# Expert stages of an eight-stage network: every token through all eight experts, or tokens sorted into tiles of 256 and sent only to their two

## Chip, cores and metric

One Trainium2 chip, one of its cores. The metric is the device time of one launch, in microseconds (us); the execution whose profile is shown lasted 3942.5 us from its first to its last instruction. A core has TensorE (PE, matrix products; PEld is its weight load), VectorE (DVE), ScalarE (ACT), GpSimd (POOL) and SyncE (SP, which here only issues transfers).

## What is computed

The input is 4 batches of 1024 tokens of 128 values. The reference is a chain of eight stages, each added to the running residual after a layer norm:

```python
x = x + attn_a(layernorm(x))         # stage 0, attention with relative positions
x = x + experts(layernorm(x))        # stage 1
x = x + mamba(layernorm(x))          # stage 2
x = x + experts(layernorm(x))        # stage 3, the same weights
x = x + sparse_attention(layernorm(x))
x = x + ffn(layernorm(x))
x = x + delta_rule(layernorm(x))
x = x + ffn(layernorm(x))

def experts(x):                       # E = 8 experts, 128 -> 2*256 -> 128, K = 2
    probs = softmax(einsum('bsh,eh->bse', x, router_w))
    weights, indices = top_k(probs, 2)
    weights = weights / (weights.sum(-1) + 1e-06)
    gate, up = split(einsum('bsh,ehi->bsei', x, w13))
    y = einsum('bsei,eih->bseh', silu(gate) * up, w2)
    return sum over the two chosen experts of weights * y
```

## The kernel before

The kernel runs the stages one after the other, each as a block of five instruction streams (one for each engine) that meet in semaphores; at the end of a block all engines meet. The residual stays in SBUF for the whole kernel, as 32 tiles of 128 tokens. Only stages 1 and 3 (`moe_stage`, called twice) and the very first loads are touched by the change.

All products of the expert stages are made of 16-bit halves: a 32-bit value is split into a high and a low f16 part, and `product_of_halves` (its matmuls are on L246) adds three matmuls: high by high, high by low, low by high.

`moe_stage` before: the tokens are taken in 8 chunks of 512, and each chunk goes through all 8 experts: 64 units. One unit is

- on PE, `up(j, 0)` and `up(j, 1)`: 12 matmuls of 512 columns (gate and value, two blocks of 128 hidden channels, three products each), then `down(j)`: 24 matmuls of 128 columns;
- on ACT, twice: the Silu of the gate (L1226) and the high half of the hidden values (`keep`, L1234);
- on DVE, twice: the product of gate and value (L1313, "exact"), and four times the weighted addition into the residual (L1324); the weight of an expert that a token didn't choose is zero;
- on POOL, twice: the low half of the hidden values (L1250).

`schedule()` is one list of pieces that every engine walks in the same order, each taking its own. `ahead(j)` slips the preparation of later batches (norm, transposes `turn`, router products `logits`, `choose`) and the splitting of the expert weights (`split`) between the units, so that the first unit starts soon after the stage does. `next_moments` takes the norm's moments for the next stage near the end. The block ends when the last addition is made.

`Net.load_rest` issues the loads that nothing at the kernel's very start needs, on SP's queue, ahead of the transfers of stage 0 (`load_psi` L654, `store_phi` L661, `store` L676, `load_phi` L669, `assemble` L691, in this order).

Of the kernel before, what the change touches and what calls it, by code (L numbers as in the profile page):

```python
# [10 lines left out]
F32 = mybir.dt.float32  # L11
BF16 = mybir.dt.bfloat16
F16 = mybir.dt.float16
U32 = mybir.dt.uint32
ALU = mybir.AluOpType
# [3 lines left out]
P = 128  # L19
# [32 lines left out]
class Net:  # L52
# [978 lines left out]
EB = HIDDEN_E // P  # L1031


def moe_stage(nc, net, name):

    with ExitStack() as stack:
        def sbuf(what, shape, dtype=F32):
            return stack.enter_context(nc.sbuf_tensor(f"{name}_{what}", shape, dtype))  # L1040

        xn = sbuf("xn", [P, TILES, P])
        xT = sbuf("xT", [P, B * T])
        probs = sbuf("probs", [P, TILES, EXPERTS])
# [3 lines left out]
        weights = sbuf("weights", [P, TILES, EXPERTS])  # L1048
# [4 lines left out]
        gate_sb = sbuf("gate", [P, 3, BANK])  # L1053
        exact_sb = sbuf("exact", [P, 3, BANK])
        hidden = sbuf("hidden", [P, 3, EB, 2, BANK], F16)
        xT_halves = sbuf("xT_halves", [P, 2, B * T], F16)
        w13_halves = sbuf("w13_halves", [P, 2, EXPERTS, 2 * HIDDEN_E], F16)
        w2_halves = sbuf("w2_halves", [P, 2, EXPERTS, EB, P], F16)
        w13 = sbuf("w13", [P, EXPERTS, 2 * HIDDEN_E])
        w2 = sbuf("w2", [P, EXPERTS, EB, P])  # L1060
        ps = stack.enter_context(nc.psum_tensor(f"{name}_ps", [P, 8, BANK], F32))
        norm = Norm(net, sbuf, (), xn, xT)
        (tokens_high, tokens_low, weights_high, weights_low, routed, shifted, raised, gate_full, value_full,
         gated, exact_made, hidden_high, hidden_low, out_full, added, step) = net.signals(
            "tokens_high tokens_low weights_high weights_low routed shifted raised gate_full value_full "
            "gated exact_made hidden_high hidden_low out_full added step")
        turned = net.signals("turned_even turned_odd")
        featured = net.signals("featured_even featured_odd")
        chunk = lambda c: slice(c * BANK, (c + 1) * BANK)
        outs = [ps[:, 6, :], ps[:, 7, :]]  # L1070
        units = CHUNKS * EXPERTS


        loads = ((0, 1), (1, 2), (2, 4), (4, EXPERTS))
        weights_in = net.signals("w_first_in w_second_in w_third_in w_rest_in")
        load_of = lambda e_: next(n for n, (_, end) in enumerate(loads) if e_ < end)

        def ahead(j):

            if j < 2:  # L1080
                yield from ([("logits", 0), ("raise", 0)], [("choose", 0, 1)])[j]
            if j + 2 < EXPERTS:
                yield "split", j + 2
            b = j // (2 * EXPERTS) + 1
            at = j % (2 * EXPERTS) - (6 if b == 1 else 2)
            if b < B:
                yield from {0: [("moments", b, 0)], 1: [("moments", b, 1)], 2: [("root", b)], 3: [("apply", b, 0)],
                            4: [("apply", b, 1)], 5: [("turn", b, 0)], 6: [("turn", b, 1)],
                            7: [("logits", b), ("raise", b)], 8: [("choose", b, 0)],
                            9: [("choose", b, 1), ("choose", b, 2)]}.get(at, ())  # L1090

        def schedule():
# [3 lines left out]
            for half in range(HALVES):  # L1096
                yield "apply", 0, half
            yield "split", 0
            yield ("ready",)
            for half in range(HALVES):  # L1100
                yield "turn", 0, half
            yield "split", 1
            for j in range(units + 2):
                if j < units:
                    yield "up", j, 0
                if j in (1, 2):
                    yield "choose", 0, 2 * j - 2
                if 1 <= j <= units:
                    yield "keep", j - 1, 1
                if j == units + 1:  # L1110
                    yield ("next_root",)
                    yield ("next_inverse",)
                if j >= 2:
                    yield "down", j - 2
                if j < units:
                    yield "up", j, 1
                    yield "keep", j, 0
                    if j >= units - 14 and j % 2 == 0 and j < units - 14 + 4 * TAKEN:
                        yield "next_moments", (j - units + 14) // 2
                    yield from ahead(j)  # L1120

        gate_ring, value_ring = Ring([ps[:, i, :] for i in (0, 2, 4)]), Ring([ps[:, i, :] for i in (1, 3, 5)])
        gate_empty = {"gate": gated, "turn": featured[0], "route": shifted}
        value_empty = {"value": exact_made, "turn": featured[1]}
        uses = {}
# [3396 lines left out]
```

## Time and profile before

| | |
|---|---|
| time, 3 runs | 3946.96 us median (3943.35 to 3953.65) |
| the profiled execution's span | 3942.5 us |
| stage 1 | 765.6 to 1054.3 us of the span |
| stage 3 | 1675.6 to 1964.9 us |
| busy over the whole span | PE 82%, DVE 72%, ACT 59%, POOL 31% |

A row of the grouped view gives the line of the kernel, the engine, what is written and read, the shape, the count, the busy time in all and the mean of one in nanoseconds, and then the engine's idle time before these instructions with what ended it. A row of the timeline gives start and length in us; one with a count merges instructions that follow each other, and its length is that of the whole run of them.

### The profile page before, as it was taken

How to read it: one execution, taken by the hardware profiler on the slowest of the kernel's cores; microseconds unless marked ns; L12 is line 12 of the kernel's file. 1: busy time of each engine (PE TensorE's matmuls, PEld its weight loads, DVE VectorE, ACT ScalarE, POOL GpSimd, SP SyncE). 2: the span in 40 equal slices, each digit the busy share in tenths (PEclk: the TensorE clock that was granted, in tenths of full speed). 3: DMA queues.
4: the chain of work that ended last, by engine and by line, in shares of the span. 5: the costliest groups of instructions: out<-in, count | busy, mean ns of one | idle time of the engine just before them, and what ended most of it. 6: DMA issues, size and time to landing. Idle time of an engine off the chain costs nothing. (4 is left out here: it accounts for less than half of the span.)

```text
span 3942.5 us, 87849 instructions
## 1 busy us (share of the span) xinstructions
PE 3249.7 (82%) x36196; PEld 1488.6 (38%) x36256; DVE 2818.9 (72%) x4293; ACT 2313.5 (59%) x3870; POOL 1237.5 (31%) x1018
## 2 busy tenths in 40 slices
PE   6999999899867677689988888887995676776799
PEld 1222222266411122156533333333453555554445
DVE  8898899587679998887746767655445667656643
ACT  3888888766444555266542566665655564543565
POOL 1100100055436776645533000001004565452100
PEclk7999999999967778799999999998997676656799
DMA  4101010100010010010036011101000000000000
GB/s 102 28 9 28 19 21 5 37 1 2 11 32 16 17 32 16 17 33 1 8 69 82 10 36 33 27 23 53 1 8 4 4 4 4 3 4 3 31 6 17
DMA packets 136019, 84.34 MB, mean 21 GB/s; under 512 B 92386, under 2 KB 107539, under 8 KB 135491
## 3 DMA queue, kind: packets, MB, share of 16 engines
q1 hardware_dynamic: 132870, 74.45, 8.7%
q0 software_dynamic: 2688, 4.20, 0.6%
q8 instruction: 289, 4.73, 0.5%
q14 instruction: 108, 0.88, 0.1%
q10 hardware_dynamic: 64, 0.07, 0.0%
HBM read 46.97 MB, written 18.33 MB: 17 GB/s over the span
## 5 line engine op out<-in xcount | busy, mean ns | idle before, releaser
L989 DVE TENSOR_REDUCE attn_peak_halves<-attn_ps 128x2 f32<-128x1024 f32 x512 | 601.5, 1218 | 58.5 <-PE attn_ps L820 50.7
L942 ACT ACTIVATE attn_weights<-attn_ps 128x512 f32<-128x512 f32 x1024 | 531.0, 601 | 101.4 <-PE attn_ps L848 101.3
L2974 DVE TENSOR_REDUCE sparse_peak<-sparse_ps 128x4 f32<-128x1024 f32 x256 | 309.6, 1223 | 136.3 <-PE sparse_ps L2600 134.5
L1250 POOL TENSOR_TENSOR moe_hidden<-moe_exact,moe_hidden 128x512 f16<-128x512 f32 x256 | 296.7, 1162 | 330.7 <-ACT moe_hidden L1234 322.0
L3672 POOL TENSOR_TENSOR delta_q<-delta_q,delta_weighted 128x512 f32<-128x512 f32 x240 | 324.1, 1377 | 235.4 <-ACT delta_weighted L4066 235.3
L2827 ACT ACTIVATE sparse_weights<-sparse_ps 128x512 f32<-128x512 f32 (+1 forms) x512 | 272.0, 585 | 173.8 <-PE sparse_ps L2667 87.9
L246 PE MATMUL moe_ps<-moe_xT_halves,moe_w_halves 128*128 128x512 f16 x1536 | 363.8, 384 | 9.4 <-DVE moe_w_halves L1267 5.9
L1772 POOL TENSOR_TENSOR mamba_out_c<-mamba_states,mamba_c_rep 128x1024 f32<-128x1024 f32 x128 | 301.4, 2367 | 176.8 <-DVE mamba_states L1839 138.5
L848 PE MATMUL attn_ps<-attn_q_stack,attn_k_stack 50*128 50x512 f16 x1024 | 321.9, 386 | 29.9 <-ACT attn_weights L942 7.1
L246 PE MATMUL ffn_ps<-ffn_layers,ffn_h_halves 128*128 128x512 f16 x1536 | 334.5, 379 | 3.6 <-ACT ffn_gate L3219 3.6
L1558 PE MATMUL mamba_ps<-mamba_stack,mamba_spread 96*128 96x512 bf16 x512 | 196.2, 493 | 157.3 <-ACT mamba_decays L1726 85.7
L1839 DVE TENSOR_TENSOR_SCAN mamba_states<-mamba_decays,mamba_ps 128x1024 f32<-128x1024 f32 x128 | 292.7, 2287 | 26.3 <-ACT mamba_decays L1726 10.1
L820 PE MATMUL attn_ps<-attn_k_stack,attn_q_stack 48*128 48x512 f16 x1024 | 271.2, 396 | 13.9 <-DVE attn_peak_halves L989 12.6
L3291 DVE TENSOR_TENSOR ffn_layers<-ffn_exact,ffn_layers 128x512 f16<-128x512 f32 x192 | 132.5, 692 | 204.8 <-ACT ffn_layers L3208 204.3
L860 PE MATMUL attn_ps<-attn_weights,attn_values 128*9 128x512 f32 x2048 | 270.3, 600 | 0.0
L1726 ACT ACTIVATE mamba_decays<-mamba_ps,mamba_rates 128x1024 f32<-128x1024 f32 x128 | 141.9, 1113 | 179.4 <-PE mamba_ps L1558 177.4
L1226 ACT ACTIVATE moe_gate<-moe_ps 128x512 f32<-128x512 f32 x256 | 152.0, 594 | 138.4 <-PE moe_ps L246 134.4
L1313 DVE SCALAR_TENSOR_TENSOR moe_exact<-moe_ps,moe_gate 128x512 f32<-128x512 f32 x256 | 174.5, 684 | 78.4 <-ACT moe_gate L1226 72.4
L848 PEld LDWEIGHTS attn_ps<-attn_q_stack,attn_k_stack 50*128 50x128 f16 x1024 | 80.6, 94 | 375.1 <-ACT attn_weights L942 284.4
L246 PEld LDWEIGHTS ffn_ps<-ffn_layers,ffn_h_halves 128*128 128x128 f16 x1536 | 149.9, 98 | 184.4 <-issue 4.5
L246 PE MATMUL moe_ps<-moe_w_halves,moe_hidden 128*128 128x128 f16 x3072 | 193.7, 220 | 18.2 <-POOL moe_hidden L1250 13.6
L246 PEld LDWEIGHTS moe_ps<-moe_xT_halves,moe_w_halves 128*128 128x128 f16 x1536 | 145.0, 99 | 164.5 <-DVE moe_w_halves L1267 8.0
(451 smaller groups left out, 6293.4 us busy)
## 6 DMA issues: line engine op xcount, KB each, us to landing
mamba_stack<-mamba_parts SPq DMA_DIRECT2D x96, 128.0 KB, 2.4
sparse_factor<-sp_factor SPq DMA_DIRECT2D x24, 256.0 KB
sp_halves<-sparse_parts SPq DMA_DIRECT2D x8, 512.0 KB, 3.1
ffn_h<-in_h SPq DMA_DIRECT2D x4, 1024.0 KB, 7.9
attn_q_stack<-attn_halves SPq DMA_DIRECT2D x96, 32.0 KB
attn_k_stack<-attn_halves SPq DMA_DIRECT2D x96, 32.0 KB
attn_halves<-attn_hp SPq DMA_DIRECT2D x8, 384.0 KB, 3.1
attn_q_stack<-attn_peak_rows SPq DMA_DIRECT2D x128, 2.0 KB
```

Of the source, the lines that this page charges most:

```text
L246: made = pe.matmul(out, a, b, start=first and i == 0, stop=last and i == 2)
L820: made = pe.matmul(use.slot[:, p, :], q_stack[rows, slot, couple, t * P:(t + 1) * P], k_stack[rows, slot, couple, half_of(keys)], start=Tr ...
L848: pe.matmul(use.slot, k_stack[rows, slot, couple, k * P:(k + 1) * P], q_stack[rows, slot, couple, half_of(half)], start=True, stop=True).t ...
L860: made = pe.matmul(out_acc[32 * h:32 * h + HD + 1, :], values[:, b % 2, k, first + h, :], weights[:, step_no(g, half, k) % 2, h, :], start ...
L942: act.activation(weights[:, at % 2, h, :], use.slot, ACT.Exp).then_inc(*key_act.one())
L989: dve.tensor_reduce(peak_halves[:, turn % PEAKS, keys, at:at + 2], use.slot, AX_X, ALU.max).then_inc(*score_dve.one())
L1250: pool.tensor_tensor(low, exact_sb[:, i % 3, :], hidden[:, i // EB % 3, i % EB, 0, :], ALU.subtract).then_inc(*hidden_low.one())
L1772: pool.tensor_tensor(out_c[:, n % PRODUCTS, :], states[:, n % HELD, :], c_rep[:, b % 2, :], ALU.mult).then_inc(*product_made.one())
L1839: dve.tensor_tensor_scan(states[:, n % HELD, :], decays[:, n % DECAYS, :], mine, 0.0, ALU.mult, ALU.add).then_inc(*scanned.one())
L2827: act.activation(weights[:, at % 2, h, begin:], use.slot[:, begin:], ACT.Exp).then_inc(*key_act.one())
L2974: dve.tensor_reduce(peak[:, at % PEAKS, unit // 2, 4 * r:4 * r + 4], use.slot.rearrange("p h (a k) -> p (h a) k", a=2), AX_X, ALU.max).the ...
L3672: pool.tensor_tensor(so_far, so_far, weighted[:, half, :], ALU.add).then_inc(*long_added.one())
```

## The change

`moe_stage` is rewritten. The tokens are now routed first, in three lots (batch 0; batches 1 and 2; batch 3). For each lot, one matmul against a triangle of ones and further ones against all ones (`rank`) count how many tokens of each expert stand before each token; `place_lot` turns that into a slot number for each of a token's two choices, each expert's list rounded up to tiles of 256 slots, and into a table that names each tile's expert. A lot of n batches has 8n + 7 tiles, whatever the routing, so there are 15 + 23 + 15 = 53 tiles.

POOL writes each tile of 128 tokens (both halves, 512 bytes a token) twice into a sorted list in DRAM with an indirect DMA (`scatter`): 64 a stage. SP loads each tile of the list (128 KB) and stores each tile of results (128 KB). After a lot's results are stored, POOL gathers them with 64 indirect DMAs a stage (`gather`), and DVE adds them into the residual (`combine`).

For one tile, PE transposes the 256 tokens by four products with the identity (`gather_tile`), makes 12 matmuls of 256 columns (`up`) and 12 of 128 (`down`). ACT copies the transposed tokens out of PSUM, makes the Silu, the high half (`high`) and the copy of the result (`keep`). DVE reads the tile's expert from the table into a register (`value_load`), copies that expert's 1536 f16 weights a partition into one of four buffers, and makes the exact product and the low half (`low`), which POOL made before.

`prepare(b)` yields apply and turn of both halves, halve, logits, raise, choose in two parts, at a lot's last batch rank and place, then weigh. In the diff below the first lines stand in `load_rest`, ahead of stage 0's transfers; `copy` and `combine` are DVE's, `scatter` is POOL's.

The core of the diff:

```diff
+        for lot in self.sorted_x:
+            n = lot.shape[0] // SLOTS_E
+            sp.dma_start(lot.rearrange("(n p s) d -> p n (s d)", p=P, s=SB), self.dram["e_zeros"].unsqueeze(1).broadcast_to(
+                [P, n, SB * 2 * P])).then_inc(*self.zeroed.dma())
...
+SLOTS_E = 256
+LOTS = ((0, 1), (1, 3), (3, 4))
+PER_EXPERT = 2 * HIDDEN_E * 2 + EB * P * 2
+lot_tiles = lambda g: (LOTS[g][1] - LOTS[g][0]) * T * 2 // SLOTS_E + EXPERTS - 1
...
         def schedule():
+            yield "moments", 0, 0
+            yield "moments", 0, 1
+            yield "root", 0
+            yield ("prepare_consts",)
+            early = [b for b in range(B) if lot_of(b) < 2]
+            for n, b in enumerate(early):
+                yield from prepare(b)
+                if n == 0:
+                    for other in range(1, B):
+                        yield "moments", other, 0
+                        yield "moments", other, 1
+                        yield "root", other
+                for e_ in range(n * EXPERTS // len(early), (n + 1) * EXPERTS // len(early)):
+                    yield "split", e_
+            late = [piece for b in range(B) if lot_of(b) >= 2 for piece in prepare(b)]
+            yield "gather_tile", 0
+            yield "copy", 0
+            yield "copy", 1
+            total_steps = MOE_TILES + 4
+            for j in range(total_steps):
+                if 1 <= j <= MOE_TILES:
+                    yield "high", j - 1
+                if 3 <= j < MOE_TILES + 3:
+                    yield "keep", j - 3
+                if j + 1 < MOE_TILES:
+                    yield "gather_tile", j + 1
+                if 1 <= j <= MOE_TILES:
+                    yield "low", j - 1
+                if j < MOE_TILES:
+                    yield "up", j
+                if j + 2 < MOE_TILES:
+                    yield "copy", j + 2
+                if 2 <= j < MOE_TILES + 2:
+                    yield "down", j - 2
+                if late and j >= 1:
+                    yield late.pop(0)
+                if j == LOT_STARTS[2] + 2:
+                    for c in range(HALVES * LOTS[0][0], HALVES * LOTS[0][1]):
+                        yield "combine", c
+            for c in range(HALVES * LOTS[0][1], CHUNKS):
+                yield "combine", c
...
+                def copy(j):
...
+                    if j >= HELD_W:
+                        dve.wait_ge(*out_full.at(j - HELD_W + 1))
+                    at = dve.value_load(expert_at[0:1, j:j + 1], min_val=0, max_val=(EXPERTS - 1) * PER_EXPERT)
+                    dve.tensor_copy(held[:, j % HELD_W, :], parts[:, bass.ds(at, PER_EXPERT)]).then_inc(*copied.one())
...
+                def scatter(b):
+                    g = lot_of(b)
+                    pool.wait_ge(*tokens_low.at(b + 1))
+                    pool.wait_ge(*placed.at(g + 1))
+                    for t in range(b * TPB, (b + 1) * TPB):
+                        for k in range(2):
+                            pool.indirect_dma_start(net.sorted_x[g], bass.IndirectOffsetOnAxis(slot_at[:, k, t:t + 1], 0),
+                                                    rows[:, t].rearrange("p h d -> p (h d)"),
+                                                    None).then_inc(*scattered[g].dma())
...
+                def combine(c):
+                    dve.wait_ge(*gathered[c].at(16 * 2 * TPC))
+                    for k in range(2):
+                        for t in range(c * TPC, (c + 1) * TPC):
+                            x = net.residual[:, t, :]
+                            made = dve.scalar_tensor_tensor(x, found[:, t, k, :], share[:, k, t:t + 1], x, ALU.mult, ALU.add)
+                        made.then_inc(*added.one())
+                        dve.wait_ge(*added.now())
```

The lists in DRAM are filled with zeros once, at the kernel's start: three DMAs, 53 tiles of 128 KB, 6.9 MB, in rows of 1 KB.

## Rows read from the trace of the kernel before

**Rows 1.** The page of the profile, its first line.

```profile
span 3942.5 us, 87849 instructions
```

**Rows 2.** Busy time by stretch, the two expert stages; behind the engines PE's granted clock.

```profile
765.60:1054.30 288.70, 269.23 (x2400) 172.28 (x2400) 224.75 (x647) 182.97 (x315) 148.34 (x128) 0.97 0.04 12
1675.60:1964.90 289.30, 269.60 (x2400) 172.85 (x2400) 224.57 (x647) 182.91 (x315) 148.33 (x128) 0.98 0.04 12
```

**Rows 3.** Groups of instructions by line and shape, stage 1.

```profile
L1313 DVE SCALAR_TENSOR_TENSOR moe_exact<-moe_ps,moe_gate 128x512 f32<-128x512 f32 x128 | 87.2, 683 | 38.7 <-ACT moe_gate L1226 35.9 <-PE moe_ps L246 2.0 <-issue 0.2
L1234 ACT ACTIVATE moe_hidden<-moe_exact 128x512 f16<-128x512 f32 x128 | 79.9, 624 | 29.8 <-DVE moe_exact L1313 29.5
L1226 ACT ACTIVATE moe_gate<-moe_ps 128x512 f32<-128x512 f32 x128 | 76.0, 594 | 69.3 <-PE moe_ps L246 67.8 <-DVE moe_exact L1313 1.0
...
L327 DVE TENSOR_SCALAR moe_xn<-residual,w_ln_moments,w_ln_inv 128x128 f32<-128x128 f32 x32 | 14.5, 514 | 0.1
L1226 ACT ACT_TABLE_LOAD x7 | 9.0, 1283 | 0.1
...
L1261 DVE TENSOR_TENSOR moe_xT_halves<-moe_xT,moe_xT_halves 128x512 f16<-128x512 f32 x8 | 5.5, 692 | 3.4 <-ACT moe_xT_halves L1214 3.4
...
L416 ACT COPY moe_xT<-moe_ps 128x512 f32<-128x512 f32 x8 | 4.6, 574 | 0.0
```

**Rows 4.** Timeline of one unit near the end of stage 1.

```profile
1035.08 2.75 PE L246 MATMUL moe_ps<-moe_xT_halves,moe_w_halves 128*128 128x512 f16 x12
...
1035.99 0.60 ACT L1226 ACTIVATE moe_gate<-moe_ps 128x512 f32<-128x512 f32 x1 [1.52 <-PE moe_ps L246]
1036.48 0.62 ACT L1234 ACTIVATE moe_hidden<-moe_exact 128x512 f16<-128x512 f32 x1
1036.68 0.69 DVE L1313 SCALAR_TENSOR_TENSOR moe_exact<-moe_ps,moe_gate 128x512 f32<-128x512 f32 x1 [0.27 <-ACT moe_gate L1226]
...
1039.01 2.75 PE L246 MATMUL moe_ps<-moe_xT_halves,moe_w_halves 128*128 128x512 f16 x12
1039.21 1.12 DVE L1324 SCALAR_TENSOR_TENSOR residual<-moe_ps,moe_weights,residual 128x128 f32<-128x128 f32 x4
```

**Rows 5.** Timeline of stage 1's first 22 us.

```profile
766.61 0.38 DVE L316 BATCH_NORM_AGGREGATE w_ln_moments<-w_ln_stats 128x2 f32<-128x6 f32 x4
...
767.79 0.38 DVE L316 BATCH_NORM_AGGREGATE w_ln_moments<-w_ln_stats 128x2 f32<-128x6 f32 x4
...
768.77 2.14 DVE L327 TENSOR_SCALAR moe_xn<-residual,w_ln_moments,w_ln_inv 128x128 f32<-128x128 f32 x8
...
777.67 1.85 PE L1158 MATMUL moe_ps<-w_router,moe_xT 128*128 128x8 f32 x16
...
786.31 0.22 DVE L1284 TENSOR_REDUCE moe_best<-moe_key 128x8 f32<-128x64 f32 x1
786.56 0.22 DVE L1285 TENSOR_TENSOR moe_chosen<-moe_key,moe_best 128x64 f32<-128x64 f32 x1
```

**Rows 6.** Timeline of POOL in stage 4: the only indirect DMAs of the kernel, two of eight.

```profile
2123.13 1.10 POOL L2424 DMA_INDIRECT sparse_gathered_k<-sp_table_k,sparse_row_at  x1 [15.36 <-DVE sparse_row_at L2966]
2124.54 1.00 POOL L2424 DMA_INDIRECT sparse_gathered_v<-sp_table_v,sparse_row_at  x1 [0.30 <-issue]
```

**Rows 7.** Groups by line and shape on DVE: its widest plain cast between SBUF tensors (stage 0).

```profile
L979 DVE CAST attn_phi_parts<-attn_sums 128x1024 f16<-128x1024 f32 x1 | 0.7, 693 | 0.0
```

**Rows 8.** Timeline of the kernel's start, SP's issues and PE's first scores of stage 0.

```profile
13.41 0.82 SPq L654 DMA_DIRECT2D attn_k_stack<-in_psi  x2
...
38.70 1.04 PE L820 MATMUL attn_ps<-attn_k_stack,attn_q_stack 48*128 48x512 f16 x4
```

**Rows 9.** Busy time by stretch while the residual is loaded; last the GB/s moved.

```profile
8.00:10.00 2.00, 0.00 (x0) 0.00 (x0) 0.75 (x4) 1.26 (x3) 0.00 (x0) 1.00 0.99 391
```

**Rows 10.** Busy time by stretch in stages 4 and 6 (PE's first, its granted clock third from last).

```profile
2220.00:2260.00 40.00, 34.35 (x423) 13.62 (x432) 27.83 (x24) 27.85 (x57) 2.53 (x9) 1.00 0.01 3
3060.00:3100.00 40.00, 24.57 (x1256) 21.26 (x1253) 24.43 (x40) 23.83 (x43) 21.02 (x15) 0.67 0.02 5
```

More of the change, by code:

```diff
@@ new lines, in moe_stage, with prepare @@
+        value_bank = lambda j: ps[:, 3 + j % 2, :]
+        out_bank = ps[:, 5, 0:SB * P]
+        span = lambda g: (LOTS[g][1] - LOTS[g][0]) * TPB
+        member_of = lambda g: member[:, LOTS[g][0] * TPB + g:LOTS[g][1] * TPB + g + 1, :]
+        rank_bank = lambda g: ps[:, 7, 0:(span(g) + 1) * EXPERTS]
+        lot_of_tile = lambda j: next(g for g in range(len(LOTS)) if j < LOT_STARTS[g + 1])
+        def prepare(b):
+            yield "apply", b, 0
+            yield "turn", b, 0
+            yield "apply", b, 1
+            yield "turn", b, 1
+            yield "halve", b
+            yield "logits", b
+            yield "raise", b
+            yield "choose", b, 0
+            yield "choose", b, 1
+            if b + 1 == LOTS[lot_of(b)][1]:
+                yield "rank", lot_of(b)
+                yield "place", lot_of(b)
+            yield "weigh", b
@@ L1111, in schedule @@
+            for c in range(HALVES * LOTS[0][1], CHUNKS):
+                yield "combine", c
+                if c == HALVES * TAKEN - 1:
                     yield ("next_root",)
                     yield ("next_inverse",)
[L1113 to L1120, printed above, removed]
@@ new lines, in gather_tile @@
+                def gather_tile(j):
+                    if j == 0:
+                        pe.wait_ge(*prepared.at(1))
+                    pe.wait_ge(*loaded[j % LOADED].at(16 * (j // LOADED + 1)))
+                    if j:
+                        pe.wait_ge(*taken.at(j))
+                    for half in range(2):
+                        for s in range(SB):
+                            at = half * SLOTS_E + s * P
+                            made = pe.matmul(ps[:, 0, at:at + P], sorted_in[:, j % LOADED, s, half * P:(half + 1) * P],
+                                             ident_half[:], start=True, stop=True)
+                    made.then_inc(*turned_tile.one())
@@ L1239, in _ @@
+                pieces = {"root": lambda b: norm.root(act, b), "prepare_consts": prepare_consts, "split": split, "turn": turn,
+                          "halve": halve, "raise": raise_, "gather_tile": gather_tile, "up": up, "high": high, "keep": keep,
+                          "next_root": lambda: norm.root_next(act)}
                 for piece, *at in schedule():
@@ L1280, in take_best @@
+                    dve.tensor_tensor(batch(left, b), found_, wide(best, b), ALU.subtract).then_inc(*shifted.one())
                 def take_best(b, source, into, top):
@@ L1336, in _ @@
+                          "logits": shift_logits, "choose": choose, "place": place_lot, "weigh": weigh, "copy": copy, "up": up,
+                          "low": low, "combine": combine, "next_inverse": lambda: norm.invert_next(dve)}
                 for piece, *at in schedule():
```

414 lines of the change are left out of this document (248 added, 166 removed).

## The prediction, made before the changed kernel was run

> **What bounds the kernel now.** I read the page first: span 3942.5 us, on one core [rows 1]; the terms below are summed against this span, and the median of the runs shown, 3946.96, is 4.5 above it. Then the busy time by stretch: the two stages that are rewritten take 288.7 and 289.3 us, and PE is busy for 269 of each at a granted clock of 0.97 to 0.98 [rows 2]. Last the timeline of one unit: from one unit's first matmul to the next one's are 3.93 us (1035.08 to 1039.01) with PE never idle [rows 4]. 64 units of 3.93 are 251.5 of the 288.7 us; the rest is the start, and units of the first chunks that wait. So the stages are bound by PE, by its columns: a unit has 12 x 512 + 24 x 128 = 9216, which makes 0.426 ns a column.
>
> **PE's work after.** A tile has 12 x 256 + 12 x 128 + 4 x 128 = 5120 columns, 2.18 us at that rate; 53 tiles are 116 us instead of 251. PE stops being the bound, and the question is what a tile costs elsewhere and how long the new start and end are.
>
> **A tile's period.** The order on ACT is high(j-1), keep(j-3), the copy of the transposed tile j+1, Silu(j). high waits for DVE's exact product, and that for the Silu, so a loop closes over two engines: Silu 0.59, hop 0.09 (1036.59 to 1036.68), exact 0.68, a like hop 0.1, high 0.62, keep, copy 0.57 [rows 3, 4]. keep has 256 columns; I take 0.36 (0.57 less half of what 512 columns cost). That sums to 3.0. But ACT starts its next instruction before the former has ended (1035.99 then 1036.48, 0.49 apart for one of 0.60 [rows 4]); with this for the three that follow without a wait it is 2.7. I take **2.8**. PE (2.18) has slack of 0.6. DVE has exact, the weights' copy and low, a 128x512 subtraction that takes 0.69 [rows 3]. The copy's width isn't in the trace: 1536 elements at the rate of the widest cast (1024 in 0.693 [rows 7]) are 1.04, if a copy among f16 goes no faster, and some 0.55 if twice as fast. That makes 1.9 to 2.4, plus what the register load shows of itself. No row shows one. Its bounds: nothing, since it can run while exact does, and 1.4, the whole pitch of an indirect DMA, the nearest thing in which a sequencer or POOL fetches indices (2123.13 to 2124.54 [rows 6]). I take 0.3 exposed, so DVE stays at or under 2.7 and the loop over ACT sets the period. With both DVE costs at their upper ends DVE needs 2.4 + 1.4 - 0.3 overlap = 3.5, and a tile's period is 3.5.
> The Trainium skill, Runtime: NRT & Kernel Launch, the breakdown of the preamble, gives about 1.3 us for a short series of register loads from HBM; no row here shows one. By it the load would show about 0.6 behind exact, and the sum would stay.
>
> **The start.** Before, the later batches' preparation ran between the units. Now three batches are prepared first, each in a chain that no other work covers. Normalising 2.1, two ACT copies 1.2 with the transposes' latency 0.5, the high half of 1024 columns 1.0 and the low half 1.2 (two of 0.69 in one), router matmuls 1.85 beside them, Exp 0.4, and 17 small DVE operations at a pitch of 0.25 [rows 3, 5]: about 12.3. At a lot's end `rank` and `place` add some 1.5 on PE and 14 operations of 0.2 to 0.3, 5 in all; `weigh` is in the 12.3 or adds 0.8. Moments of batches 1 to 3 are 6 halves of 1.18 [rows 5], 7.1; batch 0's moments and root take 3; the eight experts' splits on DVE (0.69 + 0.42 less overlap) are 8 x 1.03 = 8.2, and 1 is lost on ACT. Sum: 3 + 17.3 + 7.1 + 9.2 + 12.3 + 18.1 = 67, and 3 for the first two copies and the first gate: **70 us** until tile 0's Silu.
>
> **The loop.** 52 periods of 2.8 are **145.6**. The twelve late pieces of batch 3 stand one in a step; a DVE piece costs what it takes above a slack of some 0.7: Exp with two table loads of 1.28 [rows 3] about 2, choose 1.2 and 1.0, place 2.7, halve 0.8, logits 0.9, the others 1.9: **10.5**. The additions of chunks 0 and 1 at step 40 take DVE 2 x 3.5 (eight at 0.28 [rows 4], plus moments 1.2): **6.3** after slack. From the last Silu through exact, high, low, down and keep are **4.2**.
>
> **The end.** The last store is issued and lands in 2.8 (no row shows it; twice an indirect DMA's pitch). Only then can POOL gather lot 2: 16 indirect DMAs at a pitch of 1.35 (1.41 at the pair shown [rows 6], the others are nearer 1.3), 21.6; landing 2; eight additions 2.2: **28.9** with the block's end. Lot 1's 32 gathers (43 us) fit into the 46 between tile 37's store and the last one.
>
> Scatters: lot 0's 16 (21 us) run under the preparation of batch 1 and 2. Lot 1's 32 begin at 63 us and last 43, until 106; tile 15 is wanted at about 70 + 15 x 2.8 + 10 = 122, its load some steps earlier. Hidden, with 8 us to spare; with that cover gone each further us on POOL is one on the stage, and SP, which waits at that load, holds the stores of tiles 9 and later behind it.
>
> A stage: 70 + 145.6 + 10.5 + 6.3 + 4.2 + 28.9 = **265.5**. That saves 23.2 and 23.8.
>
> **The zeros.** 6.9 MB stand on SP's queue between the router's load and `load_psi` (13.41), and behind them wait in order psi, phi, the halves' stores and the stacks, all of stage 0's inputs. The load just before moves 391 GB/s at its best [rows 9]; DRAM to DRAM is not in the trace. 6.9 MB take 18 us at 391 and 35 at half of it; I take 24. PE's first scores run at 38.70 [rows 8], behind transposes for the other batches in PE's order; I estimate that the stacks lie ready up to 6 us before. So stage 0 and all behind it shift by **18** (12 to 35).
>
> **Sum:** 3942.5 - 47.0 + 18 = 3913.5 against its span, 3918 against the median of the runs.
>
> **The rivals.**
> (a) *A tile's period is set by DVE, and the kernel is slower.* DVE goes exact, register load, copy, low in a row. If the load can't run beside exact, or the fetch takes over 1.3, the period passes 3.08, where 52 x 2 x 0.28 eat the whole 29 us. At the upper bound of 3.5: 29 - 73 = 44 slower, 3991. For it: nothing in the trace overlaps a register load with anything; against it: DVE has 0.4 to 0.9 of slack a tile. Chance 0.25.
> (b) *POOL becomes the bound.* While POOL computed, DVE's norm instruction took 0.514 on average against 0.27 alone (2.14 for 8) [rows 3, 5]: the two engines get in each other's way, in the rows at DVE's cost. The copies may do this to POOL's indirect DMAs. If each waits out part of a copy, their pitch goes from 1.35 to 1.9: lot 1's gathers overrun by 15, lot 1's scatters by 9, while the last 16 gathers run beside no copies. 24 a stage, 48 in all: 3966. Chance 0.1.
> The Trainium skill, SBUF — State Buffer, "SBUF: two separate sides", says that a DVE copy in a two-port mode locks GpSimd out of writing the descriptors of its own DMAs. The norm row agrees that the two share something; how it strikes a DMA, no run here shows.
> (c) *PE falls to its lower clock.* A stretch of stage 4 is granted 1.00, one of stage 6, where PE is idle more between its matmuls, 0.67 [rows 10]. The loop leaves PE idle for 0.6 us in every 2.8, where before there was no gap [rows 4], and which of the two it will be like the rows don't say. At the lower level, 1.2 GHz, a tile needs 4.36, so a third of the loop there costs 17 x 1.56 = 27 a stage, 54 in all: 3972. Chance 0.12.
> (d) *No gain and no loss*: the zeros cost 34, the period 2.9: 3942.5 - 36 + 34 = 3940, as runs 3945. Chance 0.13.
> (e) The loop at its lower bound, 2.7 with the zeros at 12: 3913.5 - 10 - 6 = 3897, as runs 3902; this is in the forecast's own spread, 3890 to 3934, chance 0.4.
>
> Within 0.3% (12 us) of the median is what a measurement of this kernel can't tell from no change. The forecast's 0.4 is all faster, and half of (d) and some of (a) to (c) where they strike mildly: faster 0.5, within 0.3% 0.18, slower 0.32. The range runs from 3885 to 4000: above it are (a) with (b) or (c) together, below it a start much shorter than I sum.
>
> **What would show it.** In the trace of the changed kernel: Silu to Silu 2.8 in the middle of the loop, with ACT's high waiting for DVE's exact each time and PE idle 0.5 a tile; stage starts with tile 0's Silu at 70 us; 16 gathers in a row with every other engine idle at the end, 22 us; the first scores of stage 0 at 57 instead of 38.7; granted clock above 0.9 in the loop. Wrong it would be if DVE shows no idle time between exact and low, or an idle of over a us ahead of each copy; if POOL's indirect DMAs are spaced by more than 1.6; or if tile 15 waits for its load.

## The result, and the profile after

The changed kernel took **4106.58 us** (median of 4 runs, 4102.23 to 4108.92) beside 3947.57 for the one before (3943.35 to 3953.65): ratio 1.0403, 95% interval 1.0388 to 1.0418. The forecast was 3918, the range ended at 4000. The profiled execution has a span of 4107.0 us, 164.5 more than [rows 1]. The same kernel then took 3908 to 3910 us in three of four later measurements and 4114 in the fourth; what parts the two outcomes is what the experiments are about. One execution below, of e2 (4050 us, granted clock 0.745 where its neighbours had 0.84), ran in a slower state; it counts in e2's median and not in its ratio.

First the busy time by stretch of the changed kernel, the two expert stages, which answer to [rows 2]; the columns are window, length, PE, PEld, DVE, ACT and POOL busy with instructions, granted clock, DMA share and GB/s.

```profile
785.60:1151.40 365.80, 173.19 (x1615) 139.30 (x1615) 183.26 (x519) 129.81 (x258) 124.89 (x128) 0.69 0.24 71
...
1774.95:2138.70 363.75, 171.26 (x1615) 137.43 (x1615) 182.72 (x516) 129.36 (x258) 124.83 (x128) 0.70 0.24 71
```

The stages are 77.1 and 74.5 us longer than before, where 23 each were to be saved. The first starts 20.0 later (785.6 for 765.6), stage 2 takes 2.3 more, and stages 4 to 7 take 9.3 less (1968.3 for 1977.6), which I can't explain: 20.0 + 77.1 + 2.3 + 74.5 - 9.3 = 164.6. PE's work fell as forecast, from 269 to 173 us; none of the five engines is busy for much more than half of the stage. So the time is idle time. The groups of stage 1, with what ended the idle time ahead of each, answer to [rows 3]:

```profile
L1495 DVE SCALAR_TENSOR_TENSOR moe_exact<-moe_ps,moe_gate 128x512 f32<-128x512 f32 x53 | 36.6, 691 | 92.8 <-ACT moe_gate L1339 50.7 <-issue 32.0 <-PE moe_ps L251 5.1
L1345 ACT CAST moe_hidden<-moe_exact 128x512 f16<-128x512 f32 x53 | 32.8, 619 | 60.6 <-DVE moe_exact L1495 53.2 <-issue 5.3 <-PE moe_ps L251 2.0
L1339 ACT ACTIVATE moe_gate<-moe_ps 128x512 f32<-128x512 f32 x53 | 32.2, 608 | 35.9 <-remote 23.9 <-PE moe_ps L251 11.2
L1488 DVE COPY moe_held<-moe_parts 128x1536 f16 x53 | 29.7, 561 | 42.0 <-remote 30.5 <-issue 5.7 <-PE moe_ps L251 4.5
```

"issue" and "remote" name no engine of the kernel: nothing that the profile shows held these instructions back. The timeline shows that the idle time isn't spread over the tiles. This is PE and POOL while lot 1 is scattered, 27 us into the burst of indirect DMAs:

```profile
881.04 0.96 POOL L1369 DMA_INDIRECT sorted_x<-moe_rows,moe_slot_at  x1 [0.30 <-issue]
881.67 0.37 PE L251 MATMUL moe_ps<-moe_sorted_T,moe_held 128*128 128x256 f16 x1 [0.34 <-issue]
882.31 0.96 POOL L1369 DMA_INDIRECT sorted_x<-moe_rows,moe_slot_at  x1 [0.30 <-issue]
882.36 0.10 PEld L251 LDWEIGHTS moe_ps<-moe_sorted_T,moe_held 128*128 128x128 f16 x1 [1.29 <-issue]
883.06 0.37 PE L251 MATMUL moe_ps<-moe_sorted_T,moe_held 128*128 128x256 f16 x1 [1.02 <-issue]
883.57 0.96 POOL L1369 DMA_INDIRECT sorted_x<-moe_rows,moe_slot_at  x1 [0.30 <-issue]
884.46 0.10 PEld L251 LDWEIGHTS moe_ps<-moe_sorted_T,moe_held 128*128 128x128 f16 x1 [2.00 <-issue]
...
896.44 0.69 DVE L1495 SCALAR_TENSOR_TENSOR moe_exact<-moe_ps,moe_gate 128x512 f32<-128x512 f32 x1 [24.27 <-issue]
```

Twelve matmuls of one product, with no wait between them, take 1.5 us elsewhere in this loop; here they start multiples of some 0.7 us apart, up to 2.8, while POOL's DMAs keep their pitch of 1.27. DVE waits 24.27 us for the product. From 1003 to 1044, with POOL idle, the same trace has a tile every 2.69 us. From tile 0's Silu (860.80) to the last one's (1114.89) are 254.1 us, of which 52 x 2.69 are 140.

### The profile page after: what moved, and what is told of

The parts are those of the page before. It is cut to its first block and busy times, and to the rows that moved or that the text cites. A ratio compares the mean times of both kernels' runs of the same rounds, so it can differ in the third digit from the quotient of the medians.

```text
span 4107.0 us, 84580 instructions
## 1 busy us (share of the span) xinstructions
PE 3045.3 (74%) x34626; PEld 1417.1 (35%) x34686; DVE 2734.0 (67%) x4037; ACT 2206.7 (54%) x3756; POOL 1191.1 (29%) x1018
## 3 DMA queue, kind: packets, MB, share of 16 engines
q8 instruction: 278, 4.55, 0.5%
## 5 line engine op out<-in xcount | busy, mean ns | idle before, releaser
L853 PE MATMUL attn_ps<-attn_q_stack,attn_k_stack 50*128 50x512 f16 x1024 | 321.0, 385 | 42.1 <-DMA attn_q_stack<-attn_peak_rows 15.4
L251 PE MATMUL moe_ps<-moe_sorted_T,moe_held 128*128 128x256 f16 x1272 | 188.0, 298 | 70.7 <-issue 63.4
L1369 POOL DMA_INDIRECT sorted_x<-moe_rows,moe_slot_at x128 | 126.3, 987 | 266.2 <-DVE moe_slot_at L1471 229.1
L4249 ACT ACTIVATE delta_weighted<-delta_v,delta_fir_w 128x512 f32<-128x512 f32 x240 | 168.8, 720 | 61.2 <-POOL delta_q L3855 60.1
L1380 POOL DMA_INDIRECT moe_found<-sorted_y,moe_slot_at x128 | 123.4, 964 | 248.9 <-DMA sorted_y<-moe_y 211.7
L1495 DVE SCALAR_TENSOR_TENSOR moe_exact<-moe_ps,moe_gate 128x512 f32<-128x512 f32 x106 | 73.2, 691 | 182.6 <-issue 81.7
L251 PE MATMUL moe_ps<-moe_held,moe_hidden 128*128 128x128 f16 x1272 | 102.2, 236 | 116.7 <-ACT moe_y L1352 60.0
```

Of the source, the lines that this page charges most:

```text
L251: made = pe.matmul(out, a, b, start=first and i == 0, stop=last and i == 2)
L853: pe.matmul(use.slot, k_stack[rows, slot, couple, k * P:(k + 1) * P], q_stack[rows, slot, couple, half_of(half)], start=True, stop=True).t ...
```

## The experiments

A *measurement* below is a group of kernels run beside each other on one chip; there were seven after the first one. The theories that the expectations name: **A**, POOL's bursts of indirect DMAs keep instructions from the other engines; **B**, the tile loop starves itself, by register loads or by its loads and stores; **C**, the stalls belong to the measurement; **D**, the zeros at the start bring them about; **E**, any execution can have them; **F**, crowded DMA engines hold up the instruction transfers.

**e1: no indirect DMAs.** In place of `scatter` and `gather` (SP's loads and DVE's additions then wait for `found_set`):

```
-                for b in range(B):
-                    scatter(b)
-                for c in range(CHUNKS):
-                    gather(c)
+                pool.memset(found[:], 0.0).then_inc(*found_set.one())
```

> The changed kernel without its indirect DMAs: nothing is scattered and nothing gathered (lists hold the zeros, the two found rows of each token are zeros), everything else is issued as before. Theory A (while POOL issues indirect DMAs back to back, the other engines get no instructions and run dry some 8 to 10 us into each burst): no stall is left in the tile loop, expert stage 1 takes 75 + 53 x 2.69 + 10 + 5 + 21 = 254 us instead of 365.8, and the kernel some 2 x 110 less, about 3890. Theory B (the loop starves itself: DVE's register load, or the 128 KB loads and stores of each tile, hold up the instruction transfers): the stalls, some 90 us a stage, stay, and only the end loses its wait; stage 1 about 350 us, kernel about 4075.

Measured 3876.81 us (3869.48 to 3878.47), ratio 0.9826 (0.9806 to 0.9847); stage 1 took 251.0 us, no stall in it. B seemed refuted and A confirmed, but its neighbour said otherwise.

**e2: zeros late.** `load_rest` without its last three DMAs, and in stage 0's queue:

```
                     if piece in pieces:
                         pieces[piece](*at)
+                    if piece == "assemble" and at == [2, GROUPS - 1]:
+                        net.zero_lots(sp)
```

> The changed kernel with the three transfers of zeros moved on SP's queue from the kernel's start to behind the stack transfers of batch 2 of stage 0. Theory A and the start's price: stage 0 ends some 16 to 20 us earlier (785.6 to about 768), the two expert stages stay at 365 us, kernel 4088 to 4090. Rival: the 6.9 MB delay stage 0 wherever they stand; then the kernel stays at 4106 or the gain is under 8 us.

Measured 3896.6 us, ratio 0.9861 (0.9833 to 0.9888): some 190 to 210 less than either side had forecast. With all its indirect DMAs this kernel had no stall either (stage 1: 261.5 us).

**e3 and e4: bursts in another stage**, in the kernel before, 64 DMAs that nobody waits for:

```
+                    for n in range(64):
+                        if KIND == "plain":
+                            pool.dma_start(probe_out[n], probe_row[:]).then_inc(*probe_done.dma())
+                        else:
+                            pool.indirect_dma_start(..., bass.IndirectOffsetOnAxis(probe_at[:, n:n + 1], 0), probe_row[:], ...)
+                        if KIND == "spaced":
+                            settle(pool.memset(probe_pad[:], 0.0))
```

> The kernel before the change, with 64 extra DMAs of 64 KB that nobody waits for, issued by POOL where it is idle: in the first FFN stage (stage 5) indirect scatters back to back from about 2747 us on, in the last one (stage 7) plain DMAs on POOL's queue from about 3736 us on. Theory A: in stage 5 PE goes idle some 10 to 30 us into the 81 us burst and loses 50 to 70 us, with no instruction packet seen during the burst; if it is the software queue as such, stage 7 loses as much, if only the indirect form, nothing. Theory B: no loss in either, PE busy 0.98 as before, kernel about 3947.

> The kernel before the change, with 64 extra DMAs of 64 KB that nobody waits for: in stage 5 indirect scatters by POOL with a fill of 128 x 1024 f32 between each two (pitch some 2.3 to 2.8 us in place of 1.27), in stage 7 plain DMAs on SP's queue. Theory A, if what starves the others is that the bursts leave no gap: no loss in stage 5; if each indirect DMA holds the instruction transfers up by its own time, half of the span, 60 to 80 us, shows as lower PE share or as a smaller loss. Stage 7: no loss by any theory, since the smooth part of the tile loop ran with hardware-queue transfers at 0.33 of the DMA engines. Theory B: no loss in either, kernel about 3947.

e3 took 3948.81 us: no loss, PE as busy in the burst as without it. e4 took 3964.24, PE 81.2 of the 83 us from 2747 on, as in the kernel before (81.2); stage 5 began some 7 us later than in e3, before any of the added DMAs, so one execution of e4 tells no more than that nothing like 60 us was lost. A, as I had it, failed here as in e2. So the changed kernel itself had to be run again.

**e5 and e6: the changed kernel again, and e2's again.**

> The changed kernel again, nothing edited, beside the version with the zeros late on one chip. Theory C (the stalls of the tile loop belong to the execution or the chip, not to where the zeros stand): here too the tile loops run without stalls in most executions, stage 1 takes about 265 us, and the median is 3912 to 3920, zeros at the start and all. Theory D (the zeros at the start bring the stalls about): 4100 to 4110 as before, stage 1 about 365 us, beside 3896 for the late zeros.

> The version with the zeros moved behind the stack transfers of batch 2, again, to see how often the stalls come: theory C has the same share of executions with stalls here as in the unchanged one beside it, each such execution above 4000 us; theory D has none or few here, median 3885 to 3900, and all of them there.

e5: **3908.21 us** (3898.07 to 3911.67, 6 runs), ratio 0.9889 (0.9871 to 0.9907). e6: 3895.5 (3889.98 to 3896.48), ratio 0.9861 (0.9841 to 0.9881). C holds, D falls: the very program that had taken 4106 takes 198 less. Its two expert stages by busy time:

```profile
786.91:1048.03 261.12, 152.01 (x1615) 127.66 (x1615) 184.97 (x520) 127.81 (x258) 130.83 (x128) 0.79 0.33 99
...
1671.23:1932.43 261.20, 152.02 (x1615) 127.71 (x1615) 184.63 (x520) 127.81 (x258) 130.55 (x128) 0.79 0.33 99
```

One tile of its loop, with POOL gathering beside it:

```profile
930.75 0.61 ACT L1339 ACTIVATE moe_gate<-moe_ps 128x512 f32<-128x512 f32 x1
...
931.11 0.94 POOL L1380 DMA_INDIRECT moe_found<-sorted_y,moe_slot_at  x1 [0.30 <-issue]
...
931.39 0.69 DVE L1495 SCALAR_TENSOR_TENSOR moe_exact<-moe_ps,moe_gate 128x512 f32<-128x512 f32 x1 [0.56 <-ACT moe_gate L1339]
932.12 0.56 DVE L1488 COPY moe_held<-moe_parts 128x1536 f16 x1
932.17 0.62 ACT L1345 CAST moe_hidden<-moe_exact 128x512 f16<-128x512 f32 x1 [0.81 <-DVE moe_exact L1495]
932.36 1.14 POOL L1380 DMA_INDIRECT moe_found<-sorted_y,moe_slot_at  x1 [0.31 <-issue]
...
933.43 0.61 ACT L1339 ACTIVATE moe_gate<-moe_ps 128x512 f32<-128x512 f32 x1
```

And the DMA queues from 843 to 897 us, first in the first measurement's trace of the changed kernel, then in e5's; the columns are packets, MB and share of the 16 engines:

```profile
q0 software_dynamic: 1024, 2.10, 12.5%
q1 hardware_dynamic: 144, 0.13, 0.8%
q14 instruction: 1, 0.01, 0.1%
```

```profile
q1 hardware_dynamic: 2592, 2.36, 14.7%
q0 software_dynamic: 1024, 2.10, 12.2%
q8 instruction: 3, 0.05, 0.4%
q14 instruction: 1, 0.01, 0.0%
```

POOL moved the same 1024 packets of indirect DMAs in both. In e5 three packets of q8, the 16 KB packets of instructions, came in these 54 us; in the stalled trace none did, between 842.2 and 901.7 us. That alone can't say which is cause: an engine that stands still needs no instructions.

Counting instructions in place of time tells more. A whole trace has 278 packets of q8, one for about 250 of PE's matmuls and weight loads. These rows run from one packet to the next, the first in the stalled trace and across its burst, the second in e5 from the same packet on; behind the length stand PE's matmuls and weight loads.

```profile
842.20:901.70 59.50, 18.62 (x121) 12.53 (x122) 19.15 (x57) 11.65 (x22) 31.32 (x32) 0.56 0.12 38
```

```profile
838.70:869.20 30.50, 17.14 (x142) 14.10 (x141) 20.96 (x60) 11.98 (x24) 14.32 (x14) 0.62 0.13 41
```

e5 got through 283 of PE's instructions before its next packet came. The stalled PE had stepped through only 243 of the same ones when it got that packet, so it did not wait for it. In all traces of the changed kernel, stalled or not, late zeros and gaps too, q8's packets of stage 1's loop come within 45 instructions of the same places in PE's order. The 8 KB packets of q14 do alike: the one at 870.8 in the stalled trace came behind 892 of DVE's instructions, in e5 at 864.1 behind 893. The packets follow PE's progress; they look missing in time, and by instructions none is late.

**e7 to e9: the changed kernel a third time, and two prices of the tile loop.** e8 and e9 change these lines of `copy` (e9 drops the copy, and PE reads `parts` itself):

```
-                    at = dve.value_load(expert_at[0:1, j:j + 1], min_val=0, max_val=(EXPERTS - 1) * PER_EXPERT)
-                    dve.tensor_copy(held[:, j % HELD_W, :], parts[:, bass.ds(at, PER_EXPERT)]).then_inc(*copied.one())
+                    at = j % EXPERTS * PER_EXPERT
+                    dve.tensor_copy(held[:, j % HELD_W, :], parts[:, at:at + PER_EXPERT]).then_inc(*copied.one())
```

> The changed kernel a third time, on another chip. Theory C' (the stalls of the first measurement belong to that chip or to how the program lay in its memory): 3895 to 3920 here, stage 1 at 260 us, instruction packets seen during POOL's bursts; or again 4100 to 4110 with no instruction packet in the bursts, if this chip is like the first. Nothing between the two. Theory E (any execution can have the stalls, each burst anew): single stages with stalls, times between 3910 and 4100.

> The changed kernel with DVE's copy of each tile's weights from a fixed place (expert j mod 8 for tile j) and no register load, so that most tiles are computed with another expert's weights. If the register load was exposed by 0.3 us a tile as in the prediction's sum, the period falls from 2.69 to about 2.4 and the kernel by 2 x 53 x 0.3 = 32 us against the changed kernel; if it is hidden in DVE's wait for the Silu, as the idle of 0.08 us a copy now says, by 0 to 8 us.

> The changed kernel without the copies: PE reads the parts of expert j mod 8 where they lie, so that most tiles are computed with another expert's weights. By the prediction's loop of ACT and DVE (Silu, exact, high, keep, copy) ACT sets the period and the copy is beside it: 0 to 10 us off the kernel. If DVE's copy sets it (its 0.57 us on the chain), the period falls to about 2.15 to 2.3 and the kernel by 2 x 53 x 0.45 = 48 us.

e7: 3909.54 us, without stalls. e8: 3900.46 (ratio 0.9866, 0.9844 to 0.9888), e9: 3895.27 (0.9865, 0.9838 to 0.9892). Both began stage 1 at 777 where e7 did at 787, an execution's difference in stage 0; in stage 1 itself they took 260.5 and 257.3 us beside e7's 262.0. The Silus stand 2.69 apart in all three. So the register load costs 1.5 us a stage at most, the copy some 3, nearly all of it where late pieces crowd DVE.

**e10 and e11: both outcomes sought on another chip.**

> The changed kernel a fourth time, wherever it lands. Two outcomes are known, 3908 us and 4106 us. If it is 4106 here, the traces beside it (the version without indirect DMAs, sent along) tell whether POOL's bursts are needed for the stalls. Theory C' gives one of the two times in all its executions on this chip, theory E a mixture.

> The version without indirect DMAs on the same chip as the changed kernel: if that one runs at 4106 us here and the stalls need POOL's bursts (theory A), this one stays at 3877 us; if the stalls come without them (theory B), it is at 4050 or more. If the changed kernel runs at 3908 us here, this one is 3870 to 3880 and tells nothing new on the stalls.

3909.29 and 3882.46 us: no stalls, and nothing new but the price of the indirect DMAs without stalls, 27 us for both stages.

**e12 to e14: crowded DMA engines.** In ACT's stream, ahead of tile 2's Silu:

```
+                    if j == 2:
+                        for n in range(4):
+                            act.dma_start(net.heap[n], net.dram["x"]).then_inc(*heaped.dma())
```

> The changed kernel with four copies of the input x (2 MB each, DRAM to DRAM) issued by ACT just ahead of tile 2's Silu in both expert stages, waited for at the block's end: the 16 DMA engines are crowded while POOL scatters the second lot. Theory F (crowded DMA engines hold up the instruction transfers): for the 45 to 80 us of the copies PE steps one matmul at a time, 0.7 us or more apart, with no 16 KB instruction packet, as in the first measurement; 40 to 80 us a stage lost, kernel 3990 to 4070. Otherwise: instruction packets keep landing, late by a few us at most; the loop loses only what the tile loads come late (0 to 30 us a stage), with PE idle in whole tiles, kernel 3910 to 3970.

> The same four copies in the version without indirect DMAs (nothing scattered or gathered). Theory F without need of POOL: the same stalls as in e12, 40 to 80 us a stage above its 3877 us. If the loss of e12 is that of late tile loads: the same 0 to 30 us a stage here. If it needs POOL's bursts beside the copies: under 5 us a stage here.

> The changed kernel a fifth time beside the two: 3905 to 3912 us as in the last three measurements, or 4100 to 4110 as in the first.

This measurement had the stalls: e14, the changed kernel, took **4113.58 us** (4107.68 and 4119.49). Its neighbour e13, without indirect DMAs, took **3907.67**, and e12 4102.82 (one execution each). Stage 1 of e14, e12 and e13:

```profile
783.40:1147.00 363.60, 172.03 (x1615) 138.68 (x1615) 183.51 (x520) 129.62 (x258) 125.74 (x128) 0.69 0.24 71
```

```profile
775.90:1144.20 368.30, 173.89 (x1615) 140.82 (x1615) 183.60 (x520) 129.81 (x258) 125.15 (x128) 0.69 0.30 93
860.00:900.00 40.00, 13.93 (x92) 9.85 (x93) 8.90 (x20) 7.84 (x17) 19.78 (x21) 0.53 0.76 258
```

```profile
776.40:1045.20 268.80, 152.89 (x1615) 128.21 (x1615) 186.59 (x519) 128.19 (x258) 6.92 (x1) 0.79 0.30 96
860.00:900.00 40.00, 19.56 (x209) 16.58 (x206) 16.24 (x35) 16.19 (x31) 0.00 (x0) 0.79 0.63 204
```

The copies fill the DMA engines to 0.76 in e12 and add 4.7 us to a stage with stalls; they fill them to 0.63 in e13 and don't bring the stalls, only 18 us over e1's 251.0, in which tile loads come late. F falls. e12 and e13 differ in the indirect DMAs and what waits for them: the stalls need POOL's indirect DMAs, and they need something of the measurement too.

**e15 to e17: once more in a measurement with stalls.** e16 is e3's kernel. e17 has late zeros, and beside the tile loop:

```
+                        if sent["dmas"] % 6 == 0:
+                            for _ in range(3):
+                                pool.memset(pad[:], 0.0).then_inc(*padded.one())
+                                pool.wait_ge(*padded.now())
```

> The version with the zeros behind the stack transfers, a third time. In a measurement without stalls 3890 to 3900 us, in one with stalls 3945 + 160 - 13 = 4090 to 4095 us: the zeros' place is worth 13 us in either and has nothing to do with the stalls.

> The kernel before with 64 extra indirect scatters in stage 5 and 64 extra plain DMAs on POOL's queue in stage 7 again. If this is a measurement with stalls and POOL's bursts bring them about anywhere: PE in stage 5 drops from 0.98 to under 0.5 from some 10 to 30 us into the burst, 40 to 70 us lost, no 16 KB packet meanwhile; if only the tile loop is open to it, nothing is lost. Without stalls elsewhere in this measurement: 3945 to 3950 us, as in e3.

> The version with late zeros, and behind every sixth indirect DMA that runs beside the tile loop POOL fills a pad three times (3 x 0.97 us), so that the bursts have gaps of some 3 us every 7.6 us. Theory A with gaps as the cure: in a measurement with stalls nearly all of the 2 x 90 us come back, less the price of the gaps: 3900 to 3960 against 4092 for e15. If a burst starves the others by its DMAs' number, not for want of gaps: 4060 to 4100. In a measurement without stalls only the price shows: tile 15 waits for the second lot some 8 to 12 us longer, 3900 to 3920.

e15: 4104.29 us, 10 to 14 above what I expected; stage 1 365.9. The zeros' place has nothing to do with the stalls, and that it is worth 13 us beside them too isn't shown. e16 (one execution): **4006.27** beside 3939.25 for the kernel before. From 2765 to 2830, in the burst of stage 5, e16 and then e3:

```profile
2765.00:2830.00 65.00, 15.93 (x43) 4.11 (x41) 5.12 (x20) 8.54 (x13) 49.47 (x52) 0.58 0.16 51
```

```profile
2765.00:2830.00 65.00, 63.22 (x373) 32.46 (x372) 35.61 (x77) 44.00 (x66) 49.76 (x51) 1.00 0.17 52
```

The FFN stage has no register load, no tile load and no list, and it stalls too, from 17 us into the burst (full until 2765) to its end: 67 us lost of an 81 us burst. From 2765 to 2805 POOL's queue moved 988 packets and no instruction packet came; in e3 the same window has

```profile
q0 software_dynamic: 992, 2.03, 16.4%
q8 instruction: 2, 0.03, 0.4%
q14 instruction: 2, 0.02, 0.1%
```

Here too PE's progress explains it: from e16's q8 packet at 2742.9 to its next, at 2810.7 and inside the burst, PE ran 130 matmuls and 128 weight loads, and in e3 133 and 131 from 2742.0 to 2772.2.

The 64 plain DMAs of stage 7, on the same queue in e16, cost nothing that shows (PE was busy for 10.00 us in each 10 from 3790 to 3900 but one, at 8.22); but that burst lasts only 34 us, twice what it took to run dry.

e17: **4003.09** (ratio 1.0162, 1.0118 to 1.0206), 101 less than e15 beside it; stage 1 took 313.4 us. A burst and the gap behind it in e17's queues:

```profile
q1 hardware_dynamic: 446, 0.41, 18.0%
q0 software_dynamic: 157, 0.33, 14.4%
...
q1 hardware_dynamic: 130, 0.12, 10.7%
q0 software_dynamic: 35, 0.07, 5.9%
q8 instruction: 1, 0.02, 2.3%
```

The first pair is 890.3 to 897.6, the rest 897.6 to 901.0. The instruction packet came in this gap, but another came inside the burst before it (881.8), and the first measurement's trace has two inside its own bursts (973.3 and 1053.8), so a burst doesn't shut them out. PE's pauses lie about the bursts' ends: in the 3 us from 953 on and in those from 1023 on, with bursts that end at 954.4 and 1024.3, it was busy for 0.00 and 0.12 us, and it worked again before the gap was over. Of the 209 us between e6 and e15 the gaps give back 101, net of their own price: about half, not nearly all as expected. This tells that want of gaps is a large part of it, and that a gap of 3 us is long enough for the engines to start again.

**e18: shorter gaps, oftener** (one pad behind every third DMA).

> The version with late zeros, with one pad of 0.97 us behind every third indirect DMA that runs beside the tile loop. In a measurement with stalls: if a transfer of instructions gets through in any gap (in e17 they landed in the gaps of 3 us), 3900 to 3950 us, since none is late by more than 4 us; if a gap must be longer than about 1 us, 4050 to 4100. In a measurement without stalls: the price alone, 32 x 0.4 us for the second lot, of which some 8 us are spare, 2 x 5 us, 3900 to 3910.

3927.44 us (3914.44 to 3943.6, 10 runs), ratio 0.9945 (0.9928 to 0.9962), in a measurement in which its own trace shows no stall: stage 1 took 274.7 us, 13 over the same without gaps, so the price is 26 us for both stages, 32 by the medians of e18 and e6, and more than I gave. Whether short gaps cure stalls stays untried.

## Why the prediction was wrong

**The step that failed** is the cover of POOL's bursts: "Scatters: ... Hidden, with 8 us to spare", and of lot 1's gathers, which "fit into the 46". I priced POOL's DMAs by what they cost POOL's queue and what waits for their data. They did fit: from its first Silu to its last the loop takes 154.1 us in e5 and 155.2 in e1, which scatters nothing, and the widest spacing ahead of tile 15, between tiles 12 and 13, is 5.03 and 5.67 us. But what they cost the other engines I put at nothing, without a row for it, and in a measurement with stalls it is most of those engines' time. In stage 1, 96 of the 128 indirect DMAs run beside the loop, 96 x 1.27 = 122 us of bursts, and the loop lost 254.1 - 154.1 = 100 us against e5's. No rival of mine had this. (b) looked at the same pair from the other side: that DVE's copies slow POOL's DMAs. They do, by little: 1.14 us for a DMA beside the copy and `low`, 0.94 for the one before it; the pitch in stage 1's bursts of e5 is 1.33 on average, with single ones up to 1.86, where "wrong" began at 1.6.

That burst DMAs bring the stalls is shown (e12 beside e13, e16 beside the kernel before and e3). What carries them to the other engines is open. The engines step singly through instructions that wait for nothing in the profile, which suggests their supply of instructions; but the instruction packets of the queues are not what is late, by the counts behind e5 and e16. Whether it lies behind these packets, or in something else that all engines share, no run tells.

The Trainium skill, Runtime: NRT & Kernel Launch, "Instruction fetch mechanics", says that each sequencer streams its instructions in 16 KiB blocks over a DMA queue of its own, mostly hidden. The trace agrees: the packets of q8 have that size (278 of them, 4.55 MB), and they came on time by PE's progress, with stalls and without.

**What of the measurement brings it about is open.** Three of the eight had it, each in all its kernels with indirect bursts. e5's, e12's and e15's name the same chip number, and e5's was free of it; no other chip with a number on record had it (four measurements on three chips), and the first measurement's isn't on record. So a part of the chip in it is neither shown nor excluded. All executions here carry a granted clock, which comes from the profiler's records; whether one that isn't recorded would stall is untested. The kernel before, whose eight indirect DMAs come in pairs, shows no trace of it.

**Where nothing stalled, the sum held.** e5 took 3908, the forecast 3918, and the range holds it. It is close in part by luck: the terms missed to both sides. By its terms, from e5's trace:

- *Start, 70 us until tile 0's Silu*: 70.9 (786.91 to 857.84).
- *Period, 2.8*: 2.69, 0.01 under my lower bound, with PE's gap of 0.31 ahead of `down` for the 0.5 forecast. The loop over ACT and DVE sets it; without the copy (e9) it is the same. The DVE copy took 0.56 us, the lower of its two bounds, so f16 does go at twice the rate; the register load's exposed 0.3 was under 0.03 a tile (e8).
- *Late pieces 10.5 and additions 6.3*: Silu to Silu over the loop is 154.1, less 52 x 2.69 = 139.9, less 6.2 for the additions (975.60 to 982.68, and two tiles' spacing of 8.85 for 2.69), leaves 8.0.
- *Drain 4.2 and end 28.9*: 36.1, 3.0 too little. The additions end at 1042.46 and the stage at 1048.03; what holds it is POOL's drain.
- *A stage, 265.5*: 261.1.
- *Zeros, 18*: 21.3 in stage 0's end (20.0 in the first trace), but not as I had it. First scores at 49.1, not 57: the stacks cost 10.7, and a later wait for the peak rows, whose DMAs stand behind the stacks on SP's queue, 15.4, where it was 3.0 in the trace before. The second changes with the execution: in e8, with the same stage 0, it is 6.1, and stage 1 starts at 777. The late zeros of e2, e6 and e15 don't bring back 766 either, but 774 to 778. The two waits in the first trace, and the end of the block in e5's:

```profile
PE attn_ps L853 <- DMA attn_q_stack<-attn_peak_rows: 15.4, 1, 15.4
...
PE attn_ps L825 <- DMA attn_k_stack<-attn_halves: 10.7, 1, 10.7
```

```profile
1040.15 2.31 DVE L1509 SCALAR_TENSOR_TENSOR residual<-moe_found,moe_share,residual 128x128 f32<-128x128 f32 x8 [7.65 <-DMA moe_found<-sorted_y,moe_slot_at]
1048.39 0.06 DVE L285 MEMSET w_ln_eps<- 128x1 f32 x1 [5.93 <-PEq L1189]
```

- *Rivals*: (a) no, DVE waits 0.56 for the Silu in each tile. (c) no in the loop: the granted clock is 0.97 over e5's loop and 1.00 from 910 to 970. In the first trace's loop it is 0.76, but there as a consequence: in the stalls it is at its lower level, 1.2 GHz (0.50 from 881 to 897).

**The best version** is e6's, the zeros behind the stack transfers of batch 2: ratio 0.9861 to the kernel before where nothing stalls, 13 us under e5 beside it. With stalls it is 1.0419 (e15). Of what ran with stalls only the version with gaps came near the kernel before, and it stayed above it.

## What to carry to other kernels

Long runs of GpSimd's indirect DMAs beside a loop with many instructions are a risk that no sum over one trace shows: here they cost the kernel nothing beyond their own 27 us in four measurements, and some 200 us more in three. Keep them few, put them where the other engines have nothing to do, or, if the loop must go on, leave gaps of some 3 us every few DMAs, which here gave back half of the loss. When every engine is idle and the profile names "issue" or "remote", look at what the queues moved in that window, and count the instruction packets against the instructions executed, not against time: here they looked missing and weren't late. And measure such a kernel on several occasions before you believe either number.

## What the runs showed of the hardware that was not expected

- The stalls: in 65 us of a POOL burst PE was busy for 15.93 in e16 and 63.22 in e3, the same program. It began 17 us into the burst. In the first trace's loop the last Silus ahead of three long pauses stand at 866.7, 941.1 and 972.2, 5 to 13 us into bursts that begin at 853.9, 935.7 and 966.3; singly issued matmuls stood multiples of some 0.7 us apart.
- The 16 KB instruction packets come by PE's progress, about one for 250 of its instructions, in stalls and bursts too (two inside bursts of the first trace, 973.3 and 1053.8).
- DMA engines filled to 0.63 by hardware-queue copies don't do this (e13); of plain DMAs on POOL's queue 34 us didn't either.
- A block that ends behind POOL's indirect DMAs ends some 5.5 to 5.9 us after the last work of any engine (first trace, e2, e5, e7 to e9).
- The end of stage 0 with the zeros at the start lay at 787 in e5 and at 777 in e8, whose stage 0 is the same program; a wait of 15.6 us for a transfer in the one was 6.1 in the other.
